# Graph network sums by destination node: a chunk of edges in two parts of 13 and 12 tiles with 64-node sums each, and VectorE's registers loaded without range checks

## The reference, cut to what matters

```python
# x [12500,16]; src, dst [400000], edges sorted by dst; edge_attr_16 [400000,16]; edge_attr_2 [400000,2]
dx = maximum(edge_attr_2[:, 0], 1e-6); inv_dx = 1.0 / dx
slope_e = edge_attr_2[:, 1] * inv_dx
diff = (u[dst] - u[src]) * inv_dx[:, None]                  # u is x
d1 = segment_sum(diff, dst) - segment_sum(diff, src)
S  = segment_sum(slope_e, dst)                              # the same for all 16 features
u_next = u - clip(dt, 0.01, 2.0) * (u * d1 + g * S)
x1 = layernorm(x + u_next)
sums, counts = segment_sum(edge_attr_16, dst), segment_sum(1, dst)
out = layernorm(x1 + sums / where(counts > 0, counts, 1))
```

## Time and profile before

| what | value |
|---|---|
| median of 3 runs | 4490.79 us (4490.28 to 4492.77) |
| the profiled execution | 4491.24 us, span 4489.4 us |
| TensorE matmul busy | 4395.2 us (98%) |
| VectorE busy | 3913.8 us (87%) |
| GpSimd busy | 3323.8 us (74%) |
| ScalarE busy | 1432.0 us (32%) |

### The profile page before, as it was taken

One profiled execution on the slowest core, in us unless ns is written; L12 is line 12 of the kernel. 1 busy time (PEld: TensorE's weight loads), 2 busy tenths in 40 slices (PEclk: granted clock), 3 DMA queues, 4 the chain that ended last, 5 costly groups with the idle time before them and its releaser, 6 DMA issues. The chain is left out here.

```text
span 4489.4 us, 74223 instructions
## 1 busy us (share of the span) xinstructions
PE 4395.2 (98%) x31379; PEld 1158.4 (26%) x12630; DVE 3913.8 (87%) x8730; ACT 1432.0 (32%) x1018; POOL 3323.8 (74%) x3133
## 2 busy tenths in 40 slices
PE   4999999999999999999999999999999999999997
PEld 1222222222222222222222222222222222222222
DVE  6988888888888888888888888888888888888887
ACT  4333333333333333333333333333333333333321
POOL 7777777777777777777777777777777777777760
PEclk9999999999999999999999999999999999999998
DMA  3111111111111111111111111111111111111110
GB/s 93 36 35 35 43 37 35 35 35 42 37 35 35 35 42 37 35 35 37 42 36 35 35 42 37 35 35 35 43 37 35 35 35 42 37 35 35 35 32 8
DMA packets 210291, 167.80 MB, mean 37 GB/s; under 512 B 124650, under 2 KB 193774, under 8 KB 210024
## 3 DMA queue, kind: packets, MB, share of 16 engines
q1 hardware_dynamic: 109798, 139.79, 10.0%
q0 software_dynamic: 100000, 25.80, 6.6%
q10 hardware_dynamic: 476, 2.01, 0.1%
HBM read 164.55 MB, written 2.81 MB: 37 GB/s over the span
## 5 line engine op out<-in xcount | busy, mean ns | idle before, releaser
L662 PE MATMUL ps_src<-hi_hot,spread_lo 128*128 128x392 bf16 (+1 forms) x18750 | 4115.2, 328 | 0.0
L436 POOL DMA_INDIRECT x_src<-in_x_dram,src_i x3125 | 3317.3, 1062 | 1035.1 <-issue 876.6
L1018 DVE TENSOR_SCALAR hi_hot<-col_h,hi_f,scale 128x1564 bf16<-128x1564 f16 x3125 | 2175.0, 715 | 24.7 <-PE ps_src L662 23.5
L657 PE MATMUL ps_src<-hi_hot,spread_lo 128*128 128x392 bf16 x6250 | 2050.0, 328 | 12.9 <-DVE hi_hot L1018 10.8
L657 PEld LDWEIGHTS ps_src<-hi_hot,spread_lo 128*128 128x128 f16 x6250 | 614.9, 98 | 1720.4 <-issue 1391.8
L537 ACT ACTIVATE nodes_mem<-rel_all,row_neg 128x3200 bf16<-128x3200 f16 x125 | 370.3, 2962 | 1512.7 <-PE ps_x L599 1510.2
L610 PEld LDWEIGHTS ps_w<-dst_hots,parts 128*102 128x102 bf16 x3125 | 392.5, 127 | 939.2 <-issue 901.6
L997 DVE TENSOR_TENSOR spread_lo<-spread_lo,halves 128x640 f16<-128x640 f16 x1250 | 605.6, 493 | 8.1 <-PE ps_src L662 7.9
L599 PE MATMUL ps_x<-xwin,nodes_mem 112*128 112x48 bf16 x3125 | 580.3, 188 | 20.7 <-DVE parts L926 13.5
L610 PE MATMUL ps_w<-dst_hots,parts 128*102 128x112 bf16 x3125 | 499.7, 213 | 0.0
L599 PEld LDWEIGHTS ps_x<-xwin,nodes_mem 112*128 112x128 bf16 x3125 | 301.8, 98 | 600.9 <-issue 563.5
(11 more groups left out here) (120 smaller groups left out, 1173.7 us busy)
## 6 DMA issues: line engine op xcount, KB each, us to landing
rel_all<-rel_d SPq DMA_DIRECT2D x125, 800.0 KB
x_src<-in_x_dram,src_i POOLq DMA_INDIRECT x3125
a<-in_edge_attr_dram SPq DMA_DIRECT2D x125, 200.0 KB, 2.4
a<-in_edge_attr_dram SPq DMA_DIRECT2D x125, 25.0 KB
src_i<-in_src_dram SPq DMA_DIRECT2D x125, 12.5 KB, 1.7
dst_i<-in_dst_dram SPq DMA_DIRECT2D x125, 12.5 KB, 1.7
xwin<-xparts_d SPq DMA_DIRECT2D x125, 10.5 KB
dst_sum<-in_dst_dram SPq DMA_DIRECT2D x1, 1400.0 KB
```

The lines of the kernel that those rows point to most:

```text
L436: nc.gpsimd.indirect_dma_start(x_src[:, b, j * F:(j + 1) * F], None, x[:, :], bass.IndirectOffsetOnAxis(ap=src_i[:, b, j:j + 1], axis=0)). ...
L657: return nc.tensor.matmul(out_bank, weights, moving, start=False, stop=stop)
L662: return nc.tensor.add_instruction(mybir.InstMatmult(name=nc.get_next_instruction_name(), engine=pe.engine, start_tensor_calc=False, stop_ ...
L1018: v.tensor_scalar(hi_hot[:, slot(j), 0:HOT], col_h[:, 0:HOT], hi_f[:, b, j:j + 1], scale[:, b, j:j + 1], ALU.is_equal, ALU.mult).then_inc( ...
```

## The change

Edges of a chunk are dealt out differently: the first 1,664 go to tiles 0 to 12 (partition `p` has edges `p*13` to `p*13+12`), the other 1,536 to tiles 13 to 24 (12 on each partition). Each part has its own least `dst`, and the sum by `dst` of a part covers 64 nodes from there: the one-hot has 64 columns in place of 112, the sums lie in columns 0 to 63 and 64 to 127 of `ps_w`, and VectorE adds them in two instructions. The weights of `take_sum` are now 128 columns wide (the tile's 102, and 26 more of what lies behind; `parts_mem` has room at its end; output rows 102 to 127 are not used). The window of `take_row` stays one of 112 nodes for the chunk. A part that is wider than 64 nodes would be caught by a further window, whose count now has a table of its own, `sum_tab`; TensorE loads two registers from it at each stage's head. In the inputs drawn here the widest part spans 55 nodes (12 tiles: 50), so none is entered. The loads of `src`, `dst`, and both attributes are two DMAs each. VectorE's `load_stage` takes seven registers in place of four, without range checks; counts are masked.

```diff
+    PWIN = 64
+    JA = 13
+    PARTS = [(0, JA), (JA, J)]
...
             def load_dst(c, b):
-                sp.dma_start(dst_i[:, b, :], dst_v[ds(c, 1), :, :].rearrange("o p j -> (o p) j")).then_inc(dst_loaded[b], 16)
+                for lo, hi in PARTS:
+                    sp.dma_start(dst_i[:, b, lo:hi], part_of(dst_v, c, lo, hi, 1)).then_inc(dst_loaded[b], 16)
...
-                return nc.tensor.matmul(ps_w[0:SPL * V, 0:WIN], parts[:, j, :, :].rearrange("p k v -> p (k v)"),
-                                        hots[:, j, :], start=(j == 0), stop=(j == J - 1))
+            def part_weights(j):
+
+                return parts_mem[:, j * PARTW:j * PARTW + P]
+
+            def take_sum(j):
+
+                part = int(j >= JA)
+                lo, hi = PARTS[part]
+                return nc.tensor.matmul(ps_w[:, part * PWIN:(part + 1) * PWIN], part_weights(j), dst_of_node[:, j, :],
+                                        start=(j == lo), stop=(j == hi - 1))
...
                 if finish:
-                    span = further_rows(c + 1)
+                    further_rows(c + 1)
+                    span = further_span(pe, c + 1, sum_tab)
...
-            step(v.tensor_reduce(lim[0:C, 0:1], dst_all, AX, ALU.min))
+            for part, (lo, hi) in enumerate(PARTS):
+                step(v.tensor_reduce(part_lim[0:C, part:part + 1], dst_all[:, lo * P:hi * P], AX, ALU.min))
...
-                before_last, last, after, base = nc.values_load_multi_w_load_instructions(
-                    stage_tab[0:1, ds(s * 4, 4)], engines=[dve.engine], min_val=0, max_val=max(C * (NODES // WIN), NODES - 1))[1]
+                sums_first, sums_last, rows_first, rows_last, base, base_a, base_b = nc.values_load_multi_w_load_instructions(
+                    stage_tab[0:1, ds(s * QS, QS - 1)], engines=[dve.engine])[1]
...
                 if piece == "rel2":
-                    step(v.tensor_copy(dst_rel2[:, :, :], bc(dst_rel[:, b, :], 2, 2)))
+                    for part, (lo, hi) in enumerate(PARTS):
+                        step(v.tensor_scalar(dst_rel2[:, lo:hi, :], bc(dst_rel[:, b, lo:hi], 2, 2), bases_all[:, 1 + part, ds(n, 1)], None, ALU.subtract))
...
                     ins = v.tensor_tensor(dst_of_node[:, five, :].rearrange("p j (n t) -> p j n t", t=2),
-                                          bc(col_h[:, 0:WIN].rearrange("p (n t) -> p n t", t=2), 1, 5),
-                                          bc(dst_rel2[:, five, :], 2, WIN // 2), ALU.is_equal)
+                                          bc(col_h[:, 0:PWIN].rearrange("p (n t) -> p n t", t=2), 1, 5),
+                                          bc(dst_rel2[:, five, :], 2, PWIN // 2), ALU.is_equal)
...
-                win = dst_sum[0:SPL * V, ds(base, WIN)]
-                v.tensor_tensor(win, win, ps_w[0:SPL * V, 0:WIN], ALU.add).then_inc(win_added, 1)
-                step(v.tensor_scalar(more_rel[:, :], dst_rel[:, b, :], 0.0, None, ALU.add))
+                step(v.tensor_tensor(win_a, win_a, ps_w[0:PARTW, 0:PWIN], ALU.add))
+                step(v.tensor_scalar(far[:, :], dst_rel2[:, :, 0], float(PWIN), float(FAR), ALU.is_lt, ALU.mult))
+                dve.wait_ge(dve_step, base_step + count[0])
+                v.tensor_tensor(win_b, win_b, ps_w[0:PARTW, PWIN:2 * PWIN], ALU.add).then_inc(win_added, 1)
+                step(v.tensor_tensor(more_rel[:, :], dst_rel[:, b, :], far[:, :], ALU.add))
```

More of the change, by code:

```diff
@@ L43, in gnn_kernel @@
     assert XR == C
-    assert NODES <= 1 << 14 and WIN == 16 * 7
+    assert NODES <= 1 << 14 and WIN == 16 * 7 and PWIN == 1 << 6
+    FAR = 1 << 15
     EPS = 1e-5
@@ L584, in _ @@
             nc.tensor.matmul(ps_w[0:1, 0:C], lim[0:C, 0:1], ident[0:C, 0:C], start=True, stop=True)
-            nc.tensor.matmul(ps_w[0:1, P:P + C + 1], more_f[0:C, :], before[0:C, 0:C + 1], start=True, stop=True)
-            nc.tensor.matmul(ps_w[:, 2 * P:2 * P + C], ones[0:C, :], base_diag[0:C, 0:C], start=True, stop=True).then_inc(tab_sum, 1)
+            nc.tensor.matmul(ps_w[0:1, P:P + C + 1], more_f[0:C, 0:1], before[0:C, 0:C + 1], start=True, stop=True)
+            nc.tensor.matmul(ps_w[0:1, 2 * P:2 * P + C + 1], more_f[0:C, 1:2], before[0:C, 0:C + 1], start=True, stop=True)
+            for part in range(2):
+                nc.tensor.matmul(ps_x[0:1, 0, part * P:part * P + C], part_lim[0:C, part:part + 1], ident[0:C, 0:C], start=True, stop=True)
+            for t in range(3):
+                last = nc.tensor.matmul(ps_x[:, 1, t * P:t * P + C], ones[0:C, :], base_diag[0:C, t, 0:C], start=True, stop=True)
+            last.then_inc(tab_sum, 1)
             pe.wait_ge(gi_done, 3)
@@ L606, in take_rows, with further_sum @@
                 return last
-            def take_sum(hots, j):
-                return nc.tensor.matmul(ps_w[0:SPL * V, 0:WIN], parts[:, j, :, :].rearrange("p k v -> p (k v)"),
-                                        hots[:, j, :], start=(j == 0), stop=(j == J - 1))
-            def sums(hots):
+            def part_weights(j):
[5 more added lines that the diff above has]
+                                        start=(j == lo), stop=(j == hi - 1))
+            def further_sum():
                 for j in range(J):
-                    last = take_sum(hots, j)
+                    last = nc.tensor.matmul(ps_w[:, 0:WIN], part_weights(j), more_node[:, j, :], start=(j == 0), stop=(j == J - 1))
                 return last
@@ L635, in further_rows, with window_sums_first @@
                 further_in(pe, span, more)
-                return span
-            def window_sums(n, span, first=False):
-                pe.wait_ge(dst_hot_ready, n + 1)
-                pe.wait_ge(parts_ready, n + 1)
-                if not first:
-                    pe.wait_ge(win_added, n)
-                sums(dst_of_node).then_inc(win_sum_ready, 1)
-                further_sums(span)
+            def window_sums_first():
+                pe.wait_ge(dst_hot_ready, 1)
+                pe.wait_ge(parts_ready, 1)
+                for j in range(J):
+                    last = take_sum(j)
+                last.then_inc(win_sum_ready, 1)
+                further_sums(further_span(pe, 0, sum_tab))
             def further_sums(span):
@@ L729, in _ @@
             x_of_dst(0)
-            span = further_rows(0)
+            further_rows(0)
             pe.wait_ge(x_dst_added, 1)
@@ L733, in _ @@
             x_of_dst(1)
-            window_sums(0, span, first=True)
+            window_sums_first()
             with pe.Fori(0, C - 2) as i:
@@ L773, in _ @@
             v.memset(more_rel[:, :], 0.0).then_inc(more_b, 1)
-            step(v.memset(parts[:, :, :, :], 0.0))
+            step(v.memset(parts_mem[:, :], 0.0))
             dve.wait_ge(gi_done, 3)
@@ L969, in add_window @@
                     dve.wait_ge(win_added, n)
-                win = dst_sum[0:SPL * V, ds(base, WIN)]
-                v.tensor_tensor(win, win, ps_w[0:SPL * V, 0:WIN], ALU.add).then_inc(win_added, 1)
-                step(v.tensor_scalar(more_rel[:, :], dst_rel[:, b, :], 0.0, None, ALU.add))
+                win_a, win_b = [dst_sum[0:PARTW, ds(nc.s_assert_within(part_base, 0, NODES - 1,
+                                                                       skip_runtime_bounds_check_because="it is the least dst of a part"), PWIN)]
+                                for part_base in done["part_bases"]]
+                step(v.tensor_tensor(win_a, win_a, ps_w[0:PARTW, 0:PWIN], ALU.add))
[3 more added lines that the diff above has]
+                step(v.tensor_tensor(more_rel[:, :], dst_rel[:, b, :], far[:, :], ALU.add))
                 def more(g, first):
```

130 lines of the change are left out of this document (84 added, 46 removed).

## The result

The changed kernel takes 4440.75 us at the median of 17 runs (4431.32 to 4513.79), the kernel before beside it 4490.89 (4490.28 to 4493.37): ratio 0.9904, 95% interval 0.9888 to 0.9921, which on 4490.79 us is 4447.7 (4440.5 to 4455.3). So it is faster, as forecast, but 12 to 19 us slower than the 4429 forecast. The median itself lies inside the range of 4420 to 4447; the ratio compares means, leaving out the slowest execution, and its value lies 0.7 us above the range. What the forecast had nothing of is the spread, 82 us where the kernel before has 3. The profiled execution took 4454.08 us.

A forecast was written before the change was run, and what follows sets the result against it. TensorE was taken as the bound, at 34.99 us a chunk. From 4491.24 us, 62.3 for narrower sums came off and 0.2 was added: 4429.1, as a median 4428.7, say 4429; 8-in-10 range 4420 to 4447.

The forecast's parts named there:

- The sums' width: TensorE's 3,100 sums in the loop, 64 columns in place of 112: 20.1 ns less each, 62.3 us saved.
- the weights: Loads of the sums' weights on TensorE, 128 columns in place of 102: hidden behind the sum ahead, cost nothing.
- TensorE's register load: A second register load with four checks at each stage's head: nothing; uncovered, at most 0.73 us per chunk, 90 us.
- rival 1: TensorE's short matmuls have a price of their own: a sum saves 14.7 ns, 45.6 us in all, 4445 us; chance 0.09.
- rival 2: Wider weights also remove the 2.0 ns per matmul on TensorE: 22.0 ns saved a sum, 68 us, 4423 us; chance 0.02.
- rival 5: TensorE's second register load at a stage's head isn't covered: up to 90 us more, 4519 us; chance 0.03.
- rival 6: The weights' load bounds each sum on TensorE: 49 ns more than now, +153 us, 4644 us; chance 0.01.
- VectorE: VectorE's work per chunk: shorter one-hots -0.78 us, added pieces +0.74, so nothing; `parts` has 1.76 us cover at tile 11.
- Rival 3: VectorE's added pieces cost more and miss the deadline at tile 11: 4429 to 4495 us, singly 4475; chance 0.05.
- GpSimd: GpSimd's gathers and four more DMAs per chunk on SyncE: need 33.6 us of 34.48, 0.85 left, cost nothing.
- Rival 4: GpSimd becomes the bound, each of four added DMAs stretching a gather by 0.84 us: 247 us more, 4738 us; chance 0.03.
- Prologue: Before the loop: `src` in two DMAs delays the gathers by 0.4 us, shortened one-hots give about that back; 0.2 in the sum.

The follow-up runs named there:

- e2_one_load: The changed kernel with src, dst and both attributes loaded in one DMA each, in the old edge layout (some sums lost): 4457.33 us, ratio 0.9928.
- The head start: The changed kernel with the first 13 gathers starting behind the first half of `src`, the third chunk's waiting for TensorE once: 4446.57 us, ratio 0.9893.

## Why the prediction was right, and where it wasn't

**The sums' width, the weights, TensorE's register load: right.** 28.8 ns against 28.7; loads of 98 ns hidden behind them; good stages of 34.48 us without idle time; narrow sums alone bring 62 us, the forecast's 62.3. Rivals 1, 2, 5 and 6 are out.

**VectorE: right in its sum, and the cover held.** The one-hots gave 0.13 us each (441 to 311 ns) where 0.156 was forecast. `parts` ends 1.83 us ahead of tile 11 in a good stage (forecast 1.76), and VectorE waits 3.7 us ahead of the add. Rival 3 as written, the pieces' own cost, did not come.

**GpSimd: this step failed.** "GpSimd's own need per chunk is [...] 33.6 us [...] With a chunk of 34.48 us, 0.85 us of that is left. Cost: nothing so far." Two things were wrong in it. The need was too low: I took off all 115.8 us of waiting for TensorE, which left 0.279 us of idle time a gather, but a gather that waits for TensorE has its 0.305 us of issue within that wait. With 1.067 + 0.305 the need is 34.3 us, and 0.2 is left. And the mean of 1067 ns was taken as fixed, while it depends on where VectorE's instructions lie: 1049 to 1096 ns from 2000 to 3000 us of these kernels, which is 1.2 us a chunk and far more than the 0.2. So "cost: nothing" became late stages that took 20.3 us in the profiled execution, with GpSimd never waiting, where the forecast had it wait 0.9 us a chunk.

**Rival 4 named the right engine for a wrong reason.** It let the doubled DMAs stretch the gathers, which one load in their place refuted, and argued that a stretch by VectorE would shrink, since "there will be less" of its work. Less of it made more stretch: short one-hots alone cost 48 us. At 0.03 the rival was held too unlikely, and with the 0.84 us a load far too dear.

**Prologue: the term of 0.4 us for the second load of `src` was too small.** (The sum carried 0.2 of it, for which the text gives no reason.) The first gather starts at 7.99 us where it started at 5.86. With one load in its place, in `e2_one_load`, it started at 6.45, so the second load accounts for 1.5 of the 2.1 us:

```profile
7.99 1.13 POOL L456 DMA_INDIRECT x_src<-in_x_dram,src_i  x1 [5.45 <-DMA src_i<-in_src_dram]
```

The head start gave no fewer late stages, so these 2 us are a cost of their own and not the cause of the rest.

**The spread and the range.** A range built from prices per instruction has no term for an engine at its edge; its top, 4447, was short by 0.7 us for the ratio. That the median of 4440.75 lies within it is luck: the range was drawn up for a dearer matmul, rival 1, and that did not come.

## What to carry to other kernels

When the bound engine gets faster, write down for each other engine its need per round against the new round, counting the issue time of every instruction also where it now hides in a wait, and treat anything within 3% as a bound. Where GpSimd issues gathers back to back, their duration isn't a constant but depends on VectorE's instructions beside them, most of all on f16 products of two tensors in SBUF, so that shortening VectorE's work can lengthen the kernel; try the edit that pays alone before those that only tidy up after it. Of the versions here the narrow sums alone are the fastest at 4429 us but leave out part of the sums; of those that compute everything the changed kernel with wide one-hots, 4433.19 us, beats both kernels.

## What the runs showed that I had not expected

- A gather of 0.94 us lasted 24.56 us beside VectorE's unbroken stream of f16 products, and 0.94 beside its large one-hots.
- 0.6 us a chunk more work on VectorE gave 8 us (4441 to 4433) where the gathers were the limit, and taking such work away cost 48 us (4429 to 4477).
- A load of 128 x 25 indices split in two DMAs let the gather behind it start 1.5 us later (7.99 against 6.45), not 0.4.
- What let the kernel before stand at 3 us of spread was 0.7 us of slack a chunk on an engine whose share on the page is 74%; an engine at 76% then ran from 140 us to the end of its gathers without a single wait.
